# The first chunk's sixteen broadcast tables issued two per pipeline step of the first stage, and the first passes issued in a later step

## The reference, cut to what matters

```python
def step(h, inp):                                   # one token; h is 512 channels x 16 states
    dt_t, Bp_t, C_t, x_t = inp
    dA = jnp.exp(dt_t[..., None] * A)
    h = dA * h + (dt_t * x_t)[..., None] * Bp_t[:, None, :]
    y = jnp.einsum('bdn,bn->bd', h, C_t)
    return (h, y)

xp = jnp.einsum('bld,de->ble', x, W_x)              # x: layer norm of the input
dt = jax.nn.softplus(jnp.einsum('blr,rd->bld', xp[..., :64], W_dt) + b_dt)
B_proj, C_proj = xp[..., 64:80], xp[..., 80:96]     # 16 values each per token
x = x + layernorm(scan(layernorm(x)))               # first block
x = x + layernorm(moe(layernorm(x)))                # second: 8 experts, top 2, and a shared expert
```

## Time and profile before

| | us |
|---|---|
| median of three runs | 3647.03 (3645.42 to 3653.09) |
| the profiled execution | 3653.11 |
| its span, first to last instruction | 3651.4 |
| `prepare` in it | 0 to 198.9 |
| issues of the 16 tables, line 329 | 80.48 to 119.27 |

### The profile page before, as it was taken

One profiled execution on the slowest core, in us unless ns is written; L12 is line 12 of the kernel. 1 busy time (PEld: TensorE's weight loads), 2 busy tenths in 40 slices (PEclk: granted clock), 3 DMA queues, 4 the chain that ended last, 5 costly groups with the idle time before them and its releaser, 6 DMA issues. The chain is left out here.

```text
span 3651.4 us, 45197 instructions
## 1 busy us (share of the span) xinstructions
PE 3143.7 (86%) x15190; PEld 2580.2 (71%) x15190; DVE 1856.8 (51%) x2762; ACT 1394.6 (38%) x2475; POOL 1583.1 (43%) x1459
## 2 busy tenths in 40 slices
PE   6445698988989987989999999999999999999960
PEld 3223477777777775778888888888888888888840
DVE  6489889998899881542232222222222222223238
ACT  7445576666766762311221312212213122131114
POOL 1067787978979873420320502304214033051025
PEclk8655699999999998979999999999999999999985
DMA  6848697796886946810321302203113022031039
GB/s 231 230 153 224 188 246 193 209 257 192 235 217 207 257 139 181 249 52 18 88 64 30 109 24 63 79 15 101 53 41 99 21 72 76 9 110 44 15 125 347
DMA packets 281672, 480.08 MB, mean 131 GB/s; under 512 B 30497, under 2 KB 106097, under 8 KB 281474
## 3 DMA queue, kind: packets, MB, share of 16 engines
q1 hardware_dynamic: 223104, 296.62, 27.9%
q0 software_dynamic: 56704, 180.38, 16.7%
q10 hardware_dynamic: 1666, 0.36, 0.1%
HBM read 380.18 MB, written 97.11 MB: 131 GB/s over the span
## 5 line engine op out<-in xcount | busy, mean ns | idle before, releaser
L1419 DVE CAST hh<-h 128x512 fp32r<-128x512 f32 (+1 forms) x400 | 159.2, 398 | 1301.5 <-ACT h L1271 1295.7
L1271 ACT ACTIVATE h<-c_psH,b1e 128x512 f32<-128x512 f32 (+1 forms) x384 | 237.2, 618 | 1356.2 <-PE c_psH L1590 1328.8
L818 POOL TENSOR_TENSOR u<-dtxs,Bt 128x512 f32<-128x512 f32 x512 | 667.3, 1337 | 168.6 <-DVE b_psA L722 145.2
L722 DVE TENSOR_TENSOR_SCAN b_psA<-b_psA,carry,u 128x512 f32<-128x512 f32 x512 | 657.0, 1283 | 61.5 <-ACT b_psA L595 56.4
L1339 POOL DMA_INDIRECT xrow<-xt_d,idx x80 | 89.2, 1116 | 1099.6 <-PE c_psT L1581 603.3
L1632 PE MATMUL c_psY<-W2h,hh 128*128 128x512 f32 x1344 | 534.3, 398 | 0.1
L926 PE MATMUL b_psY<-ident,pr 128*128 128x128 f32 x2048 | 343.5, 306 | 215.0 <-DVE pr L729 197.7
L1632 PE MATMUL c_psY<-W2h,hl 128*128 128x512 f32 x1344 | 526.0, 391 | 0.0
L1632 PE MATMUL c_psY<-W2l,hh 128*128 128x512 f32 x1344 | 525.4, 391 | 0.0
L926 PEld LDWEIGHTS b_psY<-ident,pr 128*128 128x128 f32 x2048 | 263.5, 155 | 299.5 <-DVE pr L729 247.3
L729 DVE TENSOR_TENSOR pr<-b_psA,Ct 128x512 f32<-128x512 f32 x512 | 354.3, 692 | 17.9 <-DMA Ct<-bc_d 0.2
(11 more groups left out here) (251 smaller groups left out, 5596.8 us busy)
## 6 DMA issues: line engine op xcount, KB each, us to landing
w<-ws_d POOLq DMA_DIRECT2D x224, 512.0 KB, 6.8
raw<-in_w SPq DMA_DIRECT2D x256, 256.0 KB, 2.8
Bt<-bc_d SPq DMA_DIRECT2D x64, 512.0 KB
Ct<-bc_d SPq DMA_DIRECT2D x64, 512.0 KB, 24.5
y_d<-yst SPq DMA_DIRECT2D x80, 256.0 KB
xn<-in_x SPq DMA_DIRECT2D x8, 1024.0 KB, 6.3
xT_d<-xnT SPq DMA_DIRECT2D x8, 1024.0 KB, 8.5
dt_d<-a_dt SPq DMA_DIRECT2D x8, 1024.0 KB, 9.5
```

The costliest lines, as they stand in the source:

```text
L722: nc.vector.tensor_tensor_scan(psA[q][:, :], psA[q][:, :], u[g % U_RING][:, :], carry[:, k:k + 1], ALU.mult, ALU.add).then_inc(s_h, 1)
L818: nc.gpsimd.tensor_tensor(u[g % U_RING][:, :], dtx[s % 2][:, :], Bt[n // TG][:, n % TG, :], ALU.mult)\
L1271: nc.scalar.activation(h32[:, 0:n * P], psH[j % 2][:, 0:n * P], ACT.Gelu, bias=b1[:, j - 1:j]).then_inc(s_gelu, 1)
```

## The change

`load_first_scans` is cut in two. `load_first_tables(j)` issues one B and one C table and is called at the end of SP's steps 3 to 10, with j = i - 3. `load_first_passes` holds the rest, the waits for three stores of chunk 0 and the five transfers of 256 KB, and is called in step 9 behind table pair 6. Before, all 21 transfers were issued at the end of step 5. The last pair, j = 7, is issued in step 10, behind the last dt and dtx stores. Nothing waits for a table inside `prepare`; the transfers, their sizes and all other waits are the same.

```diff
-            def load_first_scans():
+            def load_first_tables(j):
                 sp.wait_ge(s_obc[0], 16)
-                for j in range(NG):
-                    load_table(sp, bc_d, early["Bt"], early["s_B"], 0, j, 0)
-                    load_table(sp, bc_d, early["Ct"], early["s_C"], NS, j, 0)
+                load_table(sp, bc_d, early["Bt"], early["s_B"], 0, j, 0)
+                load_table(sp, bc_d, early["Ct"], early["s_C"], NS, j, 0)
+
+            def load_first_passes():
                 sp.wait_ge(s_odt[0], 16)
                 sp.wait_ge(s_odx[0], 16)
                 sp.wait_ge(s_oxT[0], 16)
@@
                 if 0 <= i - 3 < NCH:
                     store_dt(i - 3)
-                if i == 5:
-                    load_first_scans()
+                if 0 <= i - 3 < NG:
+                    load_first_tables(i - 3)
+                if i == NCH + 1:
+                    load_first_passes()
```

## The result

| | before | after |
|---|---|---|
| median of seven runs, us | 3647.96 (3643.51 to 3653.95) | 3625.57 (3618.20 to 3633.95) |
| ratio, 95% interval | | 0.9933 (0.9917 to 0.9948) |
| the profiled execution, us | 3653.11 | 3627.27 |
| its span | 3651.4 | 3625.6 |
| second stage starts (SP's first issue) | 198.9 | 171.3 |

The change is faster by 19 to 30 us.

What follows compares the result with a forecast made beforehand. No engine was full in the first stage; ScalarE waited 27.0 us for a bc store queued behind the tables. Removing that wait, with all other terms at 0, gave 3647.03 - 27.0 = 3620.0 us, range 3614 to 3631.

Steps and rivals of the forecast that it cites:

- rival A: Border to the second stage waits for transfers in flight (pair 7): start at 178.4, gain 20.5, 3626.5 us; chance 0.12.
- Removed: Block in step 5 gone: ScalarE's wait on the bc store and VectorE's gap behind it vanish, -27.0 us.
- Two tables a step, issue: SP's steps 3 to 10: issuing a pair takes 0.96 + 0.94 us, at most 4.8, within 12.3 free; cost 0.
- Their moving: Queue in steps 3 to 10: 3.24 us a table, 3 us backlog over steps 3 to 5; cost 0, at most 3.
- The end of the stage: Passes moved to step 9, ahead of the last dt and dtx stores: 3.2 us to move, cost 0, at most 3.
- The stage border: Pair 7 behind the last dtx store: dtx lands at 170.1, second stage starts at 171.9; cost 0, at most 4.4.
- B: In the first stage's steps, table pairs make the queue the bound: gain 10 to 20, 3632 us; chance 0.05.
- C: First stage ends later than before, above 6.1 us a table; at 7 us a table 3660 us; chance 0.03.
- Rival D: The block in step 5 was not the cause of ScalarE's wait on bc; gap stays, 3647 us; chance 0.02.
- The sum: Whole kernel: 27.0 us gained, all other terms 0, giving 3620.0 us for the median.
- the four cases that gain: Whole kernel faster: forecast (gain 24 to 29) 0.74, A 0.12, B 0.05, the rest (gains more) 0.04; stated as 0.94.

Runs made afterwards that it cites:

- again: The changed kernel as it is, timed a second time against the kernel before: 3625.32 us against 3655.08, ratio 0.9918.

## Why the prediction was right, point by point

The forecast was 3620.0 us, a gain of 27.0; the measured ratios 0.9933 and 0.9918 are gains of 24.4 and 30.0 us. The median of 3625.57 us lies 5.6 above the forecast and 0.9 below the 3626.5 of rival A, so the time alone does not tell the two apart. The profiles do: the gap is gone whole, and the border waits for no table.

*Removed.* The gap of 27.1 us was gone entirely, the rhythm 17.1 us throughout. That the block caused it is shown twice: twelve tables leave 9.2 us of it, and the full block with a longer ring leaves 26.0 at the next store. The reason given, the place behind the tables on one queue, was only half of it: on a queue of their own the tables still cost the stores most of their rate. That nothing else hid behind it is shown by the even rhythm.

*Two tables a step, issue.* I took 1 us each and bounded by 2.4. They took 0.6 to 3.2 us each, 4.5 for the pair in step 5. The bound of 2.4 did not hold for each of them, that of 4.8 for a pair did, and it costs nothing.

*Their moving.* 3.24 us a table was a little high among stores: in steps 6 to 8 the second table of a pair landed 5.1, 6.0 and 5.6 us behind the dtx store ahead of it, where 6.5 were reckoned. The queue in steps 3 to 5 was nearly full, 0.95 to 0.98 of 1.05, and not over-full. So the landings were not 1, 2 and 3 us late but under 1 us in steps 3 and 4, and 3.5 in step 5; that the last agrees is in part luck. The cost was 0, and the two kernels with extra tables show how near the edge is.

*The end of the stage.* This term I took at 0 with a bound of 3 us, and it was mis-sized: the last dtx landed after 6.5 and 5.8 us instead of 4.6, so 1.2 to 1.9 us are paid. Part comes from the passes and pair 6 ahead (5.6 us with the passes moved away). In "again" pair 6 and the passes were through 12.0 us behind the landing of the dtx store ahead of them (152.3 to 164.3), where 6.5 + 3.2 = 9.7 was reckoned, and so 3.1 us behind the issue of the last dt store instead of 0.2 ahead of it. With the passes away the pair alone took 6.1 us (152.2 to 158.3), so it is the passes that were mis-sized, at about 5.9 us instead of 3.2 (an estimate: 12.0 - 6.1). Part comes from pair 7 behind the store. With neither around, it is 4.6. I had assumed that what stands behind a store on the queue cannot delay it.

*The stage border.* The last dtx landed at 169.5 and the second stage started at 171.3, where 170.1 and 171.9 were forecast. That is luck in part: the filling of the pipeline took 2.3 us less in this execution, which hides the 1.9. ScalarE's first weight cast came 9.1 us into the stage, as forecast. Rival A did not come in its own form: the border waits for no table in flight, since the second stage began 1.8 us behind the last dtx landing with pair 7 still moving (in "again" SP goes on at 171.26, and the pair lands at 173.5 and 176.8). But it has a true kin: the border waits for SP, and SP is held when the queue is full. In the kernel with the block last that cost some 30 us (200.6 instead of 162.7 + 5.6 + 1.8).

*Rivals B and C* did not occur at two tables. C did at four tables a step, 1 to 8 us slower, where the same sum taken with 28 tables had said 5. *Rival D* is refuted by the rows.

*The sum.* 27.1 less 1.2 to 1.9 gives 25.2 to 25.9, which is what the first stage gained (25.3 in the first profile, 26.0 in the second, from chunk 2's dt to the first scan). It lies within both intervals of the whole kernel. What single executions differ by behind the first stage, up to 10 us in the scans and 5 behind them, is larger than what is left to explain. (The chances of the four cases that gain add to 0.95, not to the 0.94 of the prediction.)

What stays open: the 1 us by which transfers behind a store delay its landing was seen in the last dtx store of three profiles (5.6 us with the block last, with the passes last and with the passes in step 5; the first of them has nothing ahead of that store), and in the dtx store of chunk 6, 5.6 us with pair 6 behind it in the change and 4.6 before. It was not taken apart.

## What to carry to other kernels

A prefetch that nobody waits for still has a price, the place of every store that is issued behind it on the same queue. Price it in queue time per transfer, not in bytes, and compare it with the free time of one pipeline step; then spread it so that each step takes only what it has room for. When a wait names a transfer, ask what stood ahead of it: a longer ring only moved the wait to the next store, and another queue won back only 3 to 11 of the 27 us, because the slow packets took their turns there as well. Keep the last stores ahead of a barrier clear on both sides, and do not let the engine that issues be held by a full queue when a barrier waits for it.

## What the runs showed of the hardware

- A broadcasting load of two 2 KB rows into 128 partitions moved at 162 GB/s (3.24 us for 512 KB), where stretches of stores moved at 408. Its packets held their engine for 0.34 us, against 0.08 for a store's.
- Two queues shared the engines by number of packets, 391 to 395 (1.43 and 0.79 MB) in 10 us, not by bytes: the stores beside the tables got 79 GB/s.
- In the kernel with the block last SP issued five passes and five tables at 0.5 to 1.2 us each; from the sixth table on an issue took 1.2 to 6.1 us, with SP standing in it; its last one ended 36 us behind the issue of the last store.
- A store of 1 MB with tables and passes right behind it landed 5.6 us after its issue, with nothing behind it 4.6.
